# Three attentions of a fused transformer kernel: heads' score products on parts of TensorE's rows, units taken in pairs

## The chip, the cores and the metric

The kernel runs on one core of a Trainium2 chip. The metric is the device time of one execution in microseconds; the lower the better. All tensors are fp32.

## The reference

Sixteen images (84 x 84) are cut into 25 patches each and joined to 77 text tokens: 102 rows of 192 numbers for each of 16 sequences. Then come four pairs of an attention-like layer and a feed-forward layer, each on a layernorm and with a residual. Three of the four are softmax attentions with 12 heads:

```python
# first attention: grouped projections, relative positions
q, k: 12 heads of 64;  v: 12 heads of 16
probs = softmax((q + r_w) @ k.T + shift((q + r_r) @ r.T));  out = probs @ v @ Wo
# second (inside a layer with a convolution and a feed-forward): 12 heads of 16
attn = softmax(q @ k.T / 4);  out = attn @ v;  x = x + out @ attn_proj_w + attn_proj_b
# third: 12 heads of 64
attn = softmax(q @ k.T / 8);  out = attn @ v @ w_o + b_o
```

The others (soft-routed experts, two top-2 expert layers, a dense layer, a last attention without softmax) aren't touched by the change.

## The kernel before

Each layer runs in four **groups** (NG) of four sequences (GB). A row block has T = 102 rows, and a group's activations stand side by side as 408 columns. An attention's work in a group is cut into 16 **units** (UNITS): unit n belongs to sequence n // 4 and holds three heads (HPU). Five engines walk the units in step, each with its own hand-written loop, tied by semaphores; nothing reorders them. The passage of one unit, with the lines of the profile:

- TensorE makes the **scores** of three heads into one PSUM bank (L1928). An fp32 product shows as two records, so a unit's scores are "x6". Here the stationary operand is QT, 128 rows, in which the heads of several units stand above one another (two units of 64 rows; in the second attention four of 32). The moving operand is KZ, in which the keys of one unit stand at their rows and the other rows are zero. So all 128 rows take part in each product.
- VectorE takes each row's minimum (L929). The scores are scaled by a negative number, hence the minimum. In the first attention it first adds the relative positions (L923).
- ScalarE makes three exponentials with their sums (L1619), VectorE the inverse sums (L935), GpSimd multiplies (L666).
- TensorE **turns** (transposes) the three heads (L1967, one record each) into a bank of TBANKS, and ScalarE copies them to PT (L1613).
- TensorE multiplies with V, the **values** (L1957), into parts of 32 or 64 columns of the array. When a bank of them is full, VectorE copies it to OT (L945), and TensorE makes the **output product** of a sequence (L1940), in three parts.

ScalarE's order in step s of its loop is: copy unit s-4 to PT, then exponentials of unit s. The change leaves it as it is:

```python
                    if 0 <= s - 4 < UNITS:
                        k = at.bank(TBANKS)
                        src = full(k)[0:T, 0:TU].rearrange("p (h t) -> p h t", h=HPU)
                        free(activation(PT[s % 2][:, 0:HPU, :], src, ACT.Copy), k)
                    if s < UNITS:
                        ...
```

TensorE's order in its step s is: scores of unit s, a part of the output product, values of unit s-5, turn of unit s-3. The scores go round three banks in the second and third attention and wait for the exponentials of the unit that had the bank; in the first they go round two and wait for the addition.

In the first attention `pos(s)` puts **pieces** of other work beside the units: the position products of this and the next group (L2018; copied by ScalarE at L1661, behind the exponentials of unit s), the next group's transposes, queries and keys (L2010). ScalarE's pieces come behind unit s's exponentials. Its last group has few of them, and VectorE has pieces of the next layer instead.

The group's front (L1837 in the second and third attention) makes queries, keys and V. ScalarE copies the keys to KZ, each unit's rows apart (L1764: twelve copies of 32 rows in the second attention). GpSimd clears KZ ahead of each attention (L678, L760, L806). L1855 is the transposes with which the next group begins.

## Time and profile before

| | us |
|---|---|
| three runs | 1655.21, 1665.26, 1647.38 |
| median | 1655.21 |
| profiled execution, its own time | 1649.25 |
| its span from first to last instruction | 1647.5 |
| TensorE busy in the span | 1426.8 (87%) |
| VectorE, ScalarE, GpSimd busy | 684.2, 664.3, 387.5 |
| mean granted TensorE clock | 0.915 |

PE is TensorE's products, PEld its weight loads, DVE VectorE, ACT ScalarE, POOL GpSimd. A TensorE record spans the product from its start until its result has landed, so records overlap, and their starts tell the pace. In brackets behind a row of the timeline stands the idle time before it and the instruction that ended it.

### The profile page before, as it was taken

To read this page: it belongs to the slowest core of one execution; us is meant where nothing else is said; L and a number is where in the kernel's file an instruction comes from. 1 tells how busy PE (TensorE), PEld (TensorE's weight loads), DVE (VectorE), ACT (ScalarE), POOL (GpSimd) and SP (SyncE) were. 2 spreads that over 40 slices of the span, in tenths; PEclk is the share of its full clock that TensorE was granted. 3 is DMA by queue.
4 is the path that set the end of the run, shared out by engine and by line. 5 is a ranking of instruction groups with operands and counts; after the bars stand their busy time and mean duration, and the time that the engine had idled before them with its cause. 6 is when DMAs were issued, how large, how long until landed. Compare 5 with 4: busy or idle time off the path is not lost.

```text
span 1647.5 us, 31617 instructions
## 1 busy us (share of the span) xinstructions
PE 1426.8 (87%) x10268; PEld 1050.3 (64%) x10268; DVE 684.2 (42%) x2126; ACT 664.3 (40%) x2241; POOL 387.5 (24%) x468
## 2 busy tenths in 40 slices
PE   5899897788779678888998998799999999989994
PEld 3556665643334456666678898376676776879993
DVE  5567766611112765444326322344343323451113
ACT  1668665320001337777531122265455442213331
POOL 5213212300000232222101565122121100024441
PEclk9899997578877799999999899799999999889997
DMA  7433432649997000000005664200000300135553
GB/s 224 125 100 103 115 90 56 235 161 418 419 417 226 5 0 1 0 0 0 0 0 144 184 198 123 61 2 0 0 0 0 134 0 0 41 118 183 184 164 106
DMA packets 94439, 178.73 MB, mean 108 GB/s; under 512 B 35578, under 2 KB 54168, under 8 KB 92704
## 3 DMA queue, kind: packets, MB, share of 16 engines
q1 hardware_dynamic: 80144, 130.65, 25.2%
q10 hardware_dynamic: 7056, 30.67, 4.5%
q0 software_dynamic: 7136, 16.10, 3.2%
q8 instruction: 57, 0.93, 0.2%
q14 instruction: 46, 0.38, 0.1%
HBM read 150.39 MB, written 26.99 MB: 108 GB/s over the span
## 4 chain that ended last, share of the span: by engine, by line
PE 61%; issue 12%; DVE 12%; ACT 6%; DMA 6%; SPq 2%; POOL 1%; DVEq 0%; ACTq 0%; POOLq 0%
PE bank L1837 15%; PE bank L2357 6%; PE bank L2343 5%; PE bank L1928 4%; DMA AREA<-in_fc 4%; PE bank L1940 4%; PE bank L1957 3%; PE bank L2347 3%; PE bank L1967 3%; PE bank L2018 2%; PE bank L1903 2%; ACT ON L1619 2%; PE bank L2010 2%; PE bank L2274 1%; DVE MXU L929 1%
## 5 line engine op out<-in xcount | busy, mean ns | idle before, releaser
L1837 PE MATMUL bank<-XT,AREA 96*128 96x408 f32 (+1 forms) x640 | 239.4, 532 | 33.1 <-ACT XT L1573 15.7
L1837 PEld LDWEIGHTS bank<-XT,AREA 96*128 96x128 f32 (+1 forms) x640 | 121.9, 196 | 139.7 <-issue 100.1
L1928 PE MATMUL bank<-KZ,QT 128*102 128x102 f32 x1152 | 140.8, 262 | 9.0 <-ACT PB L1619 5.8
L666 POOL TENSOR_TENSOR PB<-PB,RCU 102x306 f32<-102x306 f32 x96 | 69.2, 720 | 317.0 <-DVE RCU L935 316.9
L650 POOL TENSOR_TENSOR RS<-VE,expo 102x4 f32<-102x4 f32 (+1 forms) x53 | 53.0, 1000 | 376.0 <-DVE VE L875 326.3
L1928 PEld LDWEIGHTS bank<-KZ,QT 128*102 128x102 f32 x1152 | 122.4, 174 | 27.2 <-issue 18.2
L2357 PE MATMUL bank<-WM,KZ 128*128 x660 | 118.2, 327 | 0.0
L2357 PEld LDWEIGHTS bank<-WM,KZ 128*128 128x128 f32 x660 | 105.7, 190 | 0.4
L1600 ACT ACTIVATE KZ<-bank,AREA 128x128 f32<-128x128 f32 x198 | 54.8, 375 | 121.7 <-PE bank L2347 121.7
L1940 PE MATMUL bank<-AREA,OT 128*102 128x192 f32 x384 | 88.9, 345 | 11.3 <-DVE SLOTS L1291 5.2
L1957 PE MATMUL bank<-PT,V 102*32 102x102 f32 (+1 forms) x1152 | 85.9, 270 | 14.5 <-DVE OT L945 12.3
L1613 ACT ACTIVATE PT<-bank 102x306 f32<-102x306 f32 x192 | 86.5, 452 | 26.2 <-PE bank L1967 25.7
L792 POOL DMA_INDIRECT rows_out<-KZ,TARGET x66 | 66.6, 1009 | 118.9 <-DVE KZ L1436 74.5
L666 POOL TENSOR_TENSOR ON<-ON,RCU 102x306 f32<-102x306 f32 x96 | 67.0, 698 | 92.4 <-DVE RCU L935 92.1
L1619 ACT ACTIVATE PB<-bank,MXU 102x102 f32<-102x102 f32 x192 | 65.9, 378 | 53.9 <-DVE MXU L929 53.9
L2343 PE MATMUL bank<-KZ,SLOTS 128*128 128x128 f32 x660 | 84.6, 275 | 2.6 <-issue 1.9
L2343 PEld LDWEIGHTS bank<-KZ,SLOTS 128*128 128x128 f32 x660 | 82.0, 192 | 3.4 <-issue 3.4
L780 POOL DMA_INDIRECT KZ<-rows_in,TOKEN x66 | 67.6, 1024 | 54.1 <-DVE TOKEN L1413 34.6
L1571 ACT ACTIVATE XT<-bank 96x408 f32<-96x408 f32 x56 | 25.8, 501 | 133.1 <-PE bank L1855 123.9
L929 DVE TENSOR_REDUCE MXU<-bank 102x3 f32<-102x306 f32 x128 | 61.0, 477 | 42.7 <-PE bank L1928 38.3
L1957 PEld LDWEIGHTS bank<-PT,V 102*32 102x32 f32 (+1 forms) x1152 | 43.2, 118 | 53.9 <-issue 34.4
L1732 ACT ACTIVATE QT<-bank 128x512 f32<-128x512 f32 (+1 forms) x32 | 15.7, 490 | 145.0 <-PE bank L2152 145.0
(335 smaller groups left out, 2734.3 us busy)
## 6 DMA issues: line engine op xcount, KB each, us to landing
AREA<-in_fc SPq DMA_DIRECT2D x10, 1536.0 KB, 21.5
SLOTS<-in_m3w SPq DMA_DIRECT2D x33, 384.0 KB
WM<-in_fc ACTq DMA_DIRECT2D x5, 2304.0 KB, 14.5
WM<-in_fc SPq DMA_DIRECT2D x6, 1536.0 KB, 21.2
AREA<-in_fc ACTq DMA_DIRECT2D x4, 2304.0 KB, 15.2
SLOTS<-in_m1w SPq DMA_DIRECT2D x33, 256.0 KB
AREA<-pos_scratch SPq DMA_DIRECT2D x16, 459.0 KB
pos_scratch<-AREA SPq DMA_DIRECT2D x8, 913.5 KB
```

The lines of the kernel that those rows point to most:

```text
L666: pool.tensor_tensor(p, p, scale, ALU.mult).then_inc(sem["probs_ready"], 1)
L780: pool.indirect_dma_start(XG[i % XRING], None, rows_in, bass.IndirectOffsetOnAxis(ap=TOKEN[:, i:i + 1], axis=0), bounds_check=NB * T - 1, ...
L792: pool.indirect_dma_start(rows_out, bass.IndirectOffsetOnAxis(ap=TARGET[:, i:i + 1], axis=0), YO[i % YRING], None, bounds_check=2 * NB * T ...
L929: give(dve.tensor_reduce(MXU[:, n % 4, 0:HPU], scores, AX.X, ALU.min), "probs_in")
L1613: free(activation(PT[s % 2][:, 0:HPU, :], src, ACT.Copy), k)
L1619: last = activation(p, p if pos else psum[k][0:T, cols(j)], ACT.Exp, scale=-1.0, bias=MXU[:, s % 4, j:j + 1], accum_out=SMU[:, s % 4, j:j ...
L1837: last = pe.matmul(dst, lhsT, rhs, start=n == 0, stop=n == len(pieces) - 1)
L1928: last = pe.matmul(psum[k][0:T, cols(j)], QT[:, tile, cols(bb)], KALL[:, unit % per_tile * (HEADS // per_tile) + tile, cols(bb)], start=Tr ...
L1940: last = pe.matmul(psum[PROJBANK][0:T, 0:D], OT[bb % 2][:, m, :], wo[:, m, :], start=m == 0, stop=m == parts - 1)
L1957: last = pe.matmul(psum[k][row:row + rows, cols(tile)], by_head(dv)[:, bb * HEADS + h, :], PT[n % 2][:, j, :], start=True, stop=True)
L2343: pe.matmul(p[:, c], w_all[:, (j * per + m) * 128:(j * per + m + 1) * 128], x[:, 0:TILE], start=m == 0, stop=False)
L2357: last = pe.matmul(p[:, 0:D], HG[i % HRING][:, f * 128:(f + 1) * 128], w2[:, bass.ds(e, 1), f * D:(f + 1) * D].rearrange("p o d -> p (o d) ...
```

## The change

Units are taken in pairs. A head's scores use only the rows at which its unit stands (64, or 32 in the second attention), of both operands; the products of the two units of a pair alternate, and go to different banks. The keys are copied whole (KT), and the zeros, their clearing and the waits for it are gone. TensorE's loop has twelve steps of a pair: values of pair step-3, turn of pair step-2, scores of pair step, then the pieces and the output product (in two parts). The scores have four banks in the second and third attention, two in the first; the values have one bank everywhere.

```diff
@@ names
-        STEPS = UNITS + 7
         PROJBANK = OBANKS[1]
-        SCORES, VALUES = (SBANKS + XBANKS[:1], SBANKS), (OBANKS[:1] + XBANKS[1:], OBANKS[:1])
+        PAIRS = UNITS // 2
+        PAIR_STEPS = PAIRS + 4
+        SCORES, VALUES = (SBANKS + XBANKS, SBANKS), OBANKS[0]
 ...
         def proj_step(bb, i):
-            return min(UPB * bb + UPB + 6 + i, STEPS - 1)
+            return min(UPB // 2 * (bb + 1) + 3 + i, PAIR_STEPS - 1)
@@ GpSimd: ahead of the first attention; two alike ahead of the second and third go too
-            for half in range(2):
-                pool.memset(KZ[64 - 64 * half:128 - 64 * half, half, :, :], 0.0
-                            ).then_inc(sem["halves_cleared"], at.one("halves_cleared"))
-            pool.wait_ge(sem["halves_cleared"], at.now("halves_cleared"))
@@ VectorE attention
-                for s in range(STEPS + 1):
-                    n = s - 6
-                    if 0 <= n < UNITS and av_filled(dv, n % UPB):
+                for s in range(2 * PAIR_STEPS):
+                    n = s - 5
+                    if s % 2 == 0 and 0 <= n < UNITS and av_filled(dv, n % UPB):
 ...
-                        if s - 1 == proj_step(bb, 2):
+                        if s == 2 * proj_step(bb, 1) + 1:
@@ ScalarE, second attention's keys (the first and third: two copies of 64 rows become one of 128)
                 for j in range(3):
                     k = at.bank(XBANKS)
-                    src = full(k)[:, 0:TG]
-                    for u in range(UPB):
-                        rows = slice(32 * u, 32 * u + 32)
-                        last = activation(KALL[rows, 3 * u + j, :], src[rows], ACT.Identity,
-                                          bias=bqk1[rows, 3 + j:4 + j])
-                    free(last, k)
+                    free(activation(KT[:, j, :], full(k)[:, 0:TG], ACT.Identity, bias=bqk1[:, 3 + j:4 + j]), k)
@@ TensorE attention, after
+                def values(pair):
+                    f = fill_of(dv, pair[0])
+                    if pair[0] == 0:
+                        moved(*v_moved)
+                    moved(pt_moved[pair[0]], pt_moved[pair[1]])
+                    if f >= 1 and (pair[0] % UPB == 0 or av_filled(dv, pair[0] % UPB - 1)):
+                        taken(f - 1)
+                    for n in pair:
+                        for j in range(HPU):
+                            h = HPU * (n % UPB) + j
+                            row, rows, tile, _ = av_place(dv, h)
+                            last = pe.matmul(psum[VALUES][row:row + rows, cols(tile)],
+                                             by_head(dv)[:, n // UPB * HEADS + h, :], PT[n % 2][:, j, :],
+                                             start=True, stop=True)
+                    if av_filled(dv, pair[1] % UPB):
+                        last.then_inc(sem["values_ready"], 1)
+                def turn(pair):
+                    for n in pair:
+                        pe.wait_ge(sem["probs_ready"], at.take("probs_ready"))
+                        k, p = claim(TBANKS)
 ...
+                def scores(pair):
+                    bb, dk = pair[0] // UPB, 128 // per_tile
 ...
+                    for j in range(HPU):
+                        for n in pair:
+                            rows = slice(n % per_tile * dk, n % per_tile * dk + dk)
+                            tile = n % UPB // per_tile * HPU + j
+                            last = pe.matmul(psum[banks[n % len(banks)]][0:T, cols(j)], QT[rows, tile, cols(bb)],
+                                             KT[rows, tile, cols(bb)], start=True, stop=True)
 ...
+                for step in range(PAIR_STEPS):
+                    pair_of = lambda n: (2 * n, 2 * n + 1) if 0 <= n < PAIRS else None
+                    if pair_of(step - 3):
+                        values(pair_of(step - 3))
+                    if pair_of(step - 2):
+                        turn(pair_of(step - 2))
+                    if pair_of(step):
+                        scores(pair_of(step))
                     if pos:
-                        pos(s)
+                        pos(2 * step)
+                    project_values(step)
+                    if pos:
+                        pos(2 * step + 1)
```

TensorE, second attention, a step within the loop over groups, before (units; ISA and REGISTER_ALU rows are waits with computed counts):

```order
L1957 MATMUL bank<-PT,V 32x102 x3
L1964 REGISTER_ALU
L1967 MATMUL bank<-ident,ON 102x102 x3
L1925 REGISTER_ALU
L1928 MATMUL bank<-KZ,QT 102x102 x3
```

and after:

```order
L1934 MATMUL bank<-KZ,QT 102x102 x12
L1915 ISA
L1796 ISA
L1918 MATMUL bank<-ident,PB 102x102 x3
L1915 REGISTER_ALU
L1796 REGISTER_ALU
L1918 MATMUL bank<-ident,PB 102x102 x3
L1929 REGISTER_ALU x2
L1934 MATMUL bank<-KZ,QT 102x102 x6
L1807 REGISTER_ALU x4
L1906 MATMUL bank<-PT,V 32x102 x6
```

The first row is the scores of pairs 0 and 1, then come the turn of pair 0, the scores of pair 2 and the values of pair 0: what was done for one unit is now done for two at a time, and the values wait for both copies of their pair.

ScalarE, second attention, end of a group's front and begin of its units, before:

```order
L1757 ACTIVATE QT<-bank,AREA 128x408
L1764 ACTIVATE KZ<-bank,AREA 32x408 x4
L1549 REGISTER_ALU
L1764 ACTIVATE KZ<-bank,AREA 32x408 x8
L1616 ISA
```

and after, with the first exponentials and copies, which stand in the same order as before:

```order
L1740 ACTIVATE QT<-bank,AREA 128x408
L1744 ACTIVATE KZ<-bank,AREA 128x408
L1533 REGISTER_ALU
L1744 ACTIVATE KZ<-bank,AREA 128x408 x2
L1600 ISA
L1603 ACTIVATE PB,SMU<-bank,MXU 102x102 x3
L1600 REGISTER_ALU
L1603 ACTIVATE PB,SMU<-bank,MXU 102x102 x3
```

Twelve key copies have become three; the units' copies (L1597) and exponentials (L1603) haven't moved against one another.

## Rows read from the trace of the kernel before

**Rows 1.** Windows of the second and third attention: length, busy time (instructions) by engine, PEclk, DMA, GB/s
```profile
718.00:754.00 36.00, 30.69 (x293) 22.86 (x293) 15.91 (x48) 29.69 (x125) 11.14 (x16) 1.00 0.00 0
1136.00:1170.00 34.00, 31.55 (x288) 25.85 (x287) 15.88 (x44) 23.43 (x113) 11.14 (x16) 1.00 0.00 0
```

**Rows 2.** Timeline, second attention, steady units: start, length, instruction, what idle time ended on
```profile
729.10 0.43 ACT L1613 ACTIVATE PT<-bank 102x306 f32<-102x306 f32 x1
...
729.59 0.38 PE L1957 MATMUL bank<-PT,V 102*32 102x102 f32 x6 [0.18 <-ACT PT L1613]
...
730.20 0.70 PE L1928 MATMUL bank<-KZ,QT 128*102 128x102 f32 x6
...
730.37 0.46 ACT L1613 ACTIVATE PT<-bank 102x306 f32<-102x306 f32 x1
...
730.88 0.38 PE L1957 MATMUL bank<-PT,V 102*32 102x102 f32 x6
...
731.19 0.47 PE L1967 MATMUL bank<-ident,ON 102*102 102x102 f32 x3
```

**Rows 3.** Timeline, second attention's third group: first scores, and the group's end
```profile
723.80 1.69 PEld L1928 LDWEIGHTS bank<-KZ,QT 128*102 128x102 f32 x18 [0.96 <-issue]
...
751.89 0.81 PEld L1855 LDWEIGHTS bank<-ident,XN 102*96 102x96 f32 x8
```

**Rows 4.** Timeline, same group: keys copied by ACT, and the product that waited
```profile
716.46 7.28 ACT L1764 ACTIVATE KZ<-bank,AREA 32x408 f32<-32x408 f32 x12 [0.77 <-PE bank L1837]
...
718.92 1.64 PE L1837 MATMUL bank<-XT,AREA 96*128 96x408 f32 x4 [1.13 <-ACT KZ L1764]
```

**Rows 5.** Timeline, third attention: first scores, the values, the transposes behind them
```profile
1135.50 0.17 PEld L1928 LDWEIGHTS bank<-KZ,QT 128*102 128x102 f32 x1 [0.15 <-issue]
...
1144.62 0.56 PE L1957 MATMUL bank<-PT,V 102*64 102x102 f32 x6
...
1145.11 0.47 PE L1967 MATMUL bank<-ident,PB 102*102 102x102 f32 x3
```

**Rows 6.** Timeline, third attention: from scores to the next copy
```profile
1152.47 0.70 PE L1928 MATMUL bank<-KZ,QT 128*102 128x102 f32 x6
...
1153.28 0.48 DVE L929 TENSOR_REDUCE MXU<-bank 102x3 f32<-102x306 f32 x1 [1.40 <-PE bank L1928]
...
1153.79 0.35 ACT L1619 ACTIVATE PB<-bank,MXU 102x102 f32<-102x102 f32 x1 [0.68 <-DVE MXU L929]
...
1154.77 0.43 ACT L1613 ACTIVATE PT<-bank 102x306 f32<-102x306 f32 x1
```

**Rows 7.** Timeline, third attention: end of the group
```profile
1169.95 0.82 PEld L1855 LDWEIGHTS bank<-ident,XN 102*96 102x96 f32 x8
```

**Rows 8.** Timeline, first attention: a position piece
```profile
156.71 0.94 PE L2018 MATMUL bank<-AREA 64*102 64x203 f32 x8
```

**Rows 9.** Timeline, first attention's last group: values, transposes, scores of one unit
```profile
259.89 0.56 PE L1957 MATMUL bank<-PT,V 102*32 102x102 f32 x6 [3.63 <-DVE OT L945]
260.38 0.75 PE L1967 MATMUL bank<-ident,ON 102*102 102x102 f32 x3
260.93 1.24 PE L1928 MATMUL bank<-KZ,QT 128*102 128x102 f32 x6
```

**Rows 10.** Windows with the granted clock, first attention
```profile
120.00:123.00 3.00, 1.57 (x14) 1.13 (x11) 1.89 (x5) 2.14 (x9) 0.43 (x1) 1.00 0.00 0
123.00:126.00 3.00, 3.00 (x21) 2.59 (x20) 1.13 (x3) 2.05 (x9) 0.27 (x1) 0.76 0.00 0
...
276.00:280.00 4.00, 2.95 (x23) 1.69 (x20) 2.62 (x9) 1.82 (x8) 1.39 (x2) 0.50 0.00 0
```

**Rows 11.** Chain that ended last, in order of time: start, length, what
```profile
28.53 5.05 DVE XN L1068 x4
...
614.28 5.25 DVE XN L879 x4
```

**Rows 12.** Timeline, GpSimd: the clearing ahead of the second attention
```profile
614.37 4.18 POOL L760 MEMSET KZ<- 128x4896 f32 x1
```

More of the change, by code:

```diff
@@ L802, in _ @@
             expert_rows(1)
-            for r in range(YRING):
-                pool.wait_ge(sem[f"scattered{r}"], 16 * len(range(r, TILES, YRING)))
-            for half in range(2):
-                pool.memset(KZ[64 - 64 * half:128 - 64 * half, half, :, :], 0.0
-                            ).then_inc(sem["halves_cleared"], at.one("halves_cleared"))
-            pool.wait_ge(sem["halves_cleared"], at.now("halves_cleared"))
             powers(1)
@@ L1916, in taken @@
                     pe.wait_ge(sem["values_taken"], before + f + 1)
-                for s in range(STEPS):
-                    if s < UNITS:
-                        bb, unit = s // UPB, s % UPB
-                        k = banks[s % len(banks)]
-                        if s < len(banks):
-                            pe.wait_ge(sem[f"bank_free{k}"], at.now(f"bank_full{k}") + 1)
-                        else:
-                            pe.wait_ge(sem[scores_read], at.take(scores_read))
+                def values(pair):
[6 more added lines that the diff above has]
+                    for n in pair:
@@ L1968, in attention @@
                         pt_moved[n] = filled(last, k)
+                def scores(pair):
+                    bb, dk = pair[0] // UPB, 128 // per_tile
+                    for n in pair:
+                        k = banks[n % len(banks)]
+                        if n < len(banks):
+                            pe.wait_ge(sem[f"bank_free{k}"], at.now(f"bank_full{k}") + 1)
+                        else:
+                            pe.wait_ge(sem[scores_read], at.take(scores_read))
+                    for j in range(HPU):
+                        for n in pair:
+                            rows = slice(n % per_tile * dk, n % per_tile * dk + dk)
+                            tile = n % UPB // per_tile * HPU + j
+                            last = pe.matmul(psum[banks[n % len(banks)]][0:T, cols(j)], QT[rows, tile, cols(bb)],
+                                             KT[rows, tile, cols(bb)], start=True, stop=True)
+                            if j == HPU - 1:
+                                last.then_inc(sem["scores_ready"], at.one("scores_ready"))
@@ new lines, in project_values @@
+                def project_values(step):
+                    for bb in range(GB):
+                        for i in range(2):
+                            if step != proj_step(bb, i):
+                                continue
+                            if i == 0:
+                                taken(fills(dv) * (bb + 1) - 1)
+                                claim(None, PROJBANK)
+                            half = (parts + 1) // 2
+                            for m in (range(half), range(half, parts))[i]:
+                                last = pe.matmul(psum[PROJBANK][0:T, 0:D], OT[bb % 2][:, m, :], wo[:, m, :],
+                                                 start=m == 0, stop=m == parts - 1)
+                            if i == 1:
+                                filled(last, PROJBANK)
@@ L2004, in _ @@
             moved(*r_moved[-2:])
-            pe.wait_ge(sem["halves_cleared"], at.take("halves_cleared", 2))
             def project(w, p6):
```

62 lines of the change are left out of this document (6 added, 56 removed).

## The prediction

> **What bounds the kernel now.** I read first the windows of the second and third attention [rows 1]: TensorE is busy 30.7 of 36 us and 31.6 of 34, ScalarE 29.7 and 23.4. TensorE seems to bound both. The timeline tells more. In the steady part of the second attention ScalarE's copies to PT follow each other at 729.10 and 730.37, 1.27 us apart, and TensorE's values at 729.59 and 730.88, 1.29 apart [rows 2]. So there a unit costs 1.27 on ScalarE (three exponentials and a copy, nothing between) and 1.29 on TensorE: both are full, and a unit can't get much cheaper through TensorE alone. In the third ScalarE has room, and TensorE sets the pace. A group's units, from the first scores to the next group's transposes, take 751.89 - 723.80 = 28.1 us in the second attention [rows 3] and 1169.95 - 1135.50 = 34.5 in the third [rows 5, 7].
>
> What lets the engines run side by side is distance. Before, the values of a unit wait for a copy that ScalarE made well before the exponentials whose scores come next on TensorE. I look at what the pairs do to that distance, since TensorE's queue is in order: who waits for a copy holds up the scores behind it.
>
> **TensorE's own work.** A unit's scores are six records in 0.70, the last one 0.25 long [rows 6], so (0.70 - 0.25) / 5 = 0.09 apart. In the first attention's position pieces eight products of 203 columns on 64 rows, by turns on the upper and the lower rows, take 0.94 [rows 8]. At the pace of the scores, doubled for twice the columns (0.18), eight in a row would take 7 x 0.18 + 0.33 = 1.6. So products on different rows do run at the same time, and a pair's scores should take what one unit's take: some 0.78 after a change of the operand's shape (0.70 and 0.08 for the first load, an estimate). The values of a unit take 731.19 - 730.88 = 0.31 to the transposes behind them [rows 2]. In a pair two heads share a part of 32 columns instead of one, about 0.22 more: 0.53. In the third attention 1145.11 - 1144.62 = 0.49 [rows 5] becomes some 0.70. Six transposes, at 0.09 with their drain, are 0.73. Sum of a pair: 0.53 + 0.73 + 0.78 = 2.04 us in the second attention, 2.21 in the third, against 2 x 1.29 = 2.6 for two units of the second before. Taken alone the change makes TensorE faster.
>
> **The wait that it adds.** In step k+2 TensorE does the values of pair k-1, then the turn of pair k, then the scores of pair k+2. The values wait for the copy of unit 2k-1. ScalarE makes that copy just before the exponentials of unit 2k+3, then come copy 2k, exponentials 2k+4, and copy 2k+1. Exponentials 2k+4 need the scores of pair k+2, which stand on TensorE behind the values that waited for copy 2k-1. And copy 2k+1, behind exponentials 2k+4, is what the next step's values wait for. That is a closed ring with nothing to spare: copy, values, turn, scores, minimum, exponentials, copy. Four banks don't help, since the scores are held by their place in the queue. Its length:
>
> - copy's end (729.10 + 0.43) to values: 729.59 - 729.53 = 0.06 [rows 2]
> - values, turn, scores: 2.04
> - scores' end to minimum, 1153.28 - 1153.17 = 0.11, minimum 0.48, on to ScalarE 0.03, exponentials 1154.77 - 1153.79 = 0.98, copy 0.43 [rows 6]: 2.03
>
> Together 4.13 us for a pair, against 2.6 before. ScalarE has 2.54 of work in it and idles 1.6; TensorE idles 2.1. In the third attention it is 4.30.
>
> **Second attention.** From the first scores: the exponentials of units 0 to 3 run as before, then copy 0, the exponentials of unit 4 (whose scores stand behind the turn of pair 0, which waits for GpSimd's second multiplication), then copy 1, at about 7.8 us (an estimate from these durations). Five rounds of the ring to copy 11: 7.8 + 5 x 4.13 = 28.4. Then two more values-turn-copy rounds, the last values, the copy to OT and the last output product, some 6.5. That is 34.9 against 28.1: +6.8. The front gets shorter. Twelve key copies of 0.61 (7.28) held the third key product until 718.92 [rows 4]; three copies hide behind products of 1.37 (4 passes at 0.34, an estimate from 1.64 for four with their tail [rows 4]). That is worth -2.1. Net +4.7 a group, +19 for four, at full clock.
>
> **Third attention.** First part 8.2, five rounds 21.5, tail 8: 37.7 against 34.5, +3.2 a group, +13 for four. The output products now lie in TensorE's idle time, which is why it loses less. Twelve key copies of 64 rows become six there. I take them as hidden behind the front's products and give them nothing; without that cover six fewer at 0.61 [rows 4] would be worth 3.7 a group, up to -15 for four.
>
> **First attention.** There the ring has the addition in it too (0.5, an estimate by the minimum's 0.48), and the piece behind the first unit's exponentials: the second piece of a step waits for banks that ScalarE empties only then, and is itself ahead of the next values. The ring is then 4.13 + 0.5 + 0.94 for the piece [rows 8] and its copy's start, some 6.1 a pair. Pieces and units tied each other before as well (a unit's piece waits for the copies behind the last unit's exponentials), so I reckon only some 0.5 a pair more, 4 a group, of which the tail and the key copies give 1 back. +3 a group for three groups and +4 for the last, in which VectorE's pieces fall into the ring, is about +12. It is my coarsest term: between -5 and +30.
>
> **Clearing.** VectorE's normalisation ahead of the second attention lasts 5.25 for four [rows 11] while GpSimd clears KZ, 4.18 from the same moment [rows 12]; the one at the start lasts 5.05. Without the clearing some 3.5 each should go: -7, between 0 and -8. The third I take at 0, within the same bounds.
>
> **The clock.** In 120 to 123 us TensorE was busy 1.57 of 3 us, and behind that the granted clock fell to 0.76 for the next three [rows 10]. In 276 to 280 it stayed at 0.50, that is 1.2 of 2.4 GHz, with 2.95 of 4 busy [rows 10]. The ring leaves TensorE busy 2.04 of 4.13, so I expect that it falls. At 1.2 GHz a unit's values, turn and scores take 0.49, 0.55 and 1.24 [rows 9]; for a pair I make 0.83 + 1.24 + 1.24 = 3.3, and the ring is 5.4. Low throughout, a group of the second attention gets 5 x 1.27 longer, its tail and the next front some 6 more: +17, +68 for four. In the third the output products would fill TensorE's idle time and may bring the clock back: low for three rounds +6 a group, throughout +15. I take half of the low price in the second, 4 x 11 = +44, and +24 in the third.
>
> **Sum.** 12 + 44 + 24 - 7 = +73 on the profiled execution's 1649.25: 1722. The median of the runs is 6 above it and their spread 18, so I say 1725.
>
> **Rivals.**
>
> - *The clock holds.* 12 + 19 + 13 - 7 = +37: 1686. For it: 2.1 us of idle time in each ring is broken up by output products from the fifth step on. Against: [rows 10].
> - *The clock is low throughout*, in the first attention also (25): 25 + 68 + 60 - 7 = +146: 1795.
> - *Rows don't run together.* The change then doesn't do what it says. A pair's scores cost 0.54 more in the ring, about 20 rings a stage (five to seven in four groups) and three stages: 75 x 0.54 = 40 more, 1765. [Rows 8] speak against it.
> - *The ring doesn't close, ScalarE becomes the bound, and it is faster.* If copies ran far enough ahead of the values, a pair would cost ScalarE's 2.54: the second attention keeps its pace and gains the front's 2.1 and some 3 of output products, 5 x 4 = 20; the third would come to about 27, 7.5 x 4 = 30; the first 8, the clearing 7: -65, 1584. It decides itself at 2.6 us a pair; the ring would have to lose 1.5, and its parts outside TensorE alone are 2.1. For it: TensorE's sum of 2.04. Against: the order of ScalarE's loop, which is unchanged.
>
> On this last rival bears the Trainium skill, page "TensorEngine Tiling (Array Packing)", section "PSUM Bottleneck": tiling speeds up TensorE but not the emptying of PSUM, which may become the bottleneck. By that rule the second attention would stand at ScalarE's 1.27 a unit, with no loss; the trace shows ScalarE full already, and my ring says that it will have gaps instead.
>
> **Chances.** A measurement of this kernel tells about 1% from no change. Ring with a mixed clock 0.52 (1700 to 1755); clock holds 0.20 (1670 to 1700); low throughout 0.12 (1755 to 1800); no concurrency 0.04; ring much shorter or made up elsewhere, within 1%, 0.08; faster by over 1% 0.04. The range leaves out the fastest and part of the slowest: 1665 to 1790. Slower by over 1%: 0.88.
>
> **What would show it.** In the trace of after: in the second attention, copies to PT in groups of two about 4.1 us (or 5.4) apart in steady steps; ScalarE idle until VectorE's minimum, once a pair; TensorE idle until ScalarE's copy ahead of the values; a pair's scores in 0.8 us, with two banks' records starting together; PEclk under 1.00 there; ScalarE's busy share down. The first key copy of the second attention followed at once by products; no 5 us normalisation at 28 and 614. Wrong would prove me scores that don't wait behind the values, or a ring under 3 us.

## The result, and the profile after

| | before | after |
|---|---|---|
| median of the runs, us | 1657.7 (1647.38 to 1665.26) | 1775.31 |
| ratio, 95% interval | | 1.0703 (1.0624 to 1.0782) |
| profiled execution: its own time, span | 1649.25, 1647.5 | 1769.63, 1767.9 |
| mean granted TensorE clock | 0.915 | 0.834 |

The change makes the kernel 7% slower. One execution of after took 3294.63 us and is left out of the ratio, though not of the median; the three others took 1769.63 to 1776.12.

I cut both spans at the first attention's first scores (L1928 before, L1934 after) and, for the second and third attention, at the transposes (L1855, L1831) with which their first group begins; each attention ends at the first transposes behind its last group. All in us:

| stretch | before | after | more | predicted |
|---|---|---|---|---|
| to the first attention's first scores | 62.6 | 55.7 | -6.9 | -3.5 |
| first attention | 225.8 | 258.6 | +32.8 | +12 |
| to the second attention | 331.3 | 328.9 | -2.4 | -3.5 |
| second attention | 175.3 | 232.1 | +56.8 | +44 |
| to the third | 245.8 | 248.3 | +2.5 | 0 |
| third attention | 254.4 | 295.7 | +41.3 | +24 |
| rest | 352.3 | 348.6 | -3.7 | 0 |
| sum | | | +120.4 | +73 |

Windows of after over a group's units, second and third attention; columns as in [rows 1], to which they answer (the engines stand there in the order PE, PEld, DVE, ACT, POOL):

```profile
656.00:701.00 45.00, 32.31 (x265) 23.75 (x264) 14.03 (x41) 23.88 (x113) 11.13 (x16) 0.58 0.01 1
1156.00:1200.00 44.00, 32.14 (x284) 25.75 (x283) 15.81 (x44) 23.65 (x113) 11.14 (x16) 0.73 0.00 1
```

Before, TensorE and ScalarE had little room in the second attention: they were busy 30.69 and 29.69 of 36 us. Now TensorE is busy 32.31 of 45 and ScalarE 23.88, and the granted clock is 0.58 and 0.73 in place of 1.00. Both engines idle, so something waits in turn. The timeline of the second attention of after, rows of one round and the start of the next (they answer to [rows 2, 6]):

```profile
724.94 1.36 PE L1934 MATMUL bank<-KZ,QT 32*102 32x102 f32 x12
726.40 0.48 DVE L914 TENSOR_REDUCE MXU<-bank 102x3 f32<-102x306 f32 x1 [3.57 <-PE bank L1934]
...
726.91 0.35 ACT L1603 ACTIVATE ON<-bank,MXU 102x102 f32<-102x102 f32 x1 [1.95 <-DVE MXU L914]
...
727.89 0.43 ACT L1597 ACTIVATE PT<-bank 102x306 f32<-102x306 f32 x1
...
728.37 0.89 PE L1906 MATMUL bank<-PT,V 102*32 102x102 f32 x12 [2.07 <-ACT PT L1597]
...
729.19 1.26 PE L1918 MATMUL bank<-ident,PB 102*102 102x102 f32 x6
...
730.38 1.36 PE L1934 MATMUL bank<-KZ,QT 32*102 32x102 f32 x12
731.84 0.48 DVE L914 TENSOR_REDUCE MXU<-bank 102x3 f32<-102x306 f32 x1 [2.06 <-PE bank L1934]
...
733.89 0.90 PE L1906 MATMUL bank<-PT,V 102*32 102x102 f32 x12 [2.15 <-ACT PT L1597]
```

Read it as a circle. ScalarE idles 1.95 until VectorE's minimum; VectorE waited for the scores, and those stood on TensorE behind the values, which idled 2.07 until ScalarE's copy. The values come 733.89 - 728.37 = 5.52 us apart for a pair, against 2 x 1.29 before. The pair's twelve score records end in 1.36 together. In the chain that ended last the same beat shows (start, length, what):

```profile
665.52 3.53 issue
...
670.98 3.53 issue
...
676.43 3.60 issue
```

670.98 - 665.52 = 5.46. Between these rows stand only GpSimd's multiplications and short pieces of issue, no output product and no DMA. In the third attention the beat is 5.92 (values at 1170.43 and 1176.35). The normalisations of [rows 11] no longer run beside a clearing. Before, one of the four instructions at 614.28 took 4.38 us, the others 0.37 each, while GpSimd cleared KZ from 614.37 for 4.18 [rows 12]. Now:

```profile
28.05 1.40 DVE L1053 TENSOR_SCALAR XN<-H,MV,RS 102x192 f32<-102x192 f32 x4 [1.15 <-POOL RS L650]
...
641.80 1.25 DVE L864 TENSOR_SCALAR XN<-SLOTS,MV,RS 102x192 f32<-102x192 f32 x4 [1.12 <-POOL RS L650]
```

### The profile page after: what moved, and what is told of

Its sections match the earlier page's. It is cut to its first block, busy times and chain, and to the rows that moved or that the text cites. A ratio compares the mean times of both kernels' runs of the same rounds, so it can differ in the third digit from the quotient of the medians.

```text
span 1767.9 us, 31591 instructions
## 1 busy us (share of the span) xinstructions
PE 1454.3 (82%) x10268; PEld 1076.5 (61%) x10268; DVE 669.1 (38%) x2114; ACT 630.3 (36%) x2169; POOL 374.7 (21%) x463
## 4 chain that ended last, share of the span: by engine, by line
PE 42%; issue 32%; DVE 8%; DMA 6%; ACT 5%; POOL 4%; SPq 2%; POOLq 0%; DVEq 0%; ACTq 0%
PE bank L2349 6%; PE bank L1813 5%; DMA WM<-in_fc 5%; PE bank L2335 4%; PE bank L1934 4%; PE bank L1918 3%; PE bank L2339 3%; PE bank L2006 3%; PE bank L1906 2%; PE bank L2014 2%; POOL PB L666 1%; DVE MXU L914 1%; ACT ON L1603 1%; ACT PB L1603 1%; PE bank L1950 1%
## 5 line engine op out<-in xcount | busy, mean ns | idle before, releaser
L1906 PE MATMUL bank<-PT,V 102*32 102x102 f32 (+1 forms) x1152 | 81.4, 330 | 84.6 <-ACT PT L1597 82.3
L1906 PEld LDWEIGHTS bank<-PT,V 102*32 102x32 f32 (+1 forms) x1152 | 53.4, 150 | 123.4 <-issue 93.3
L1934 PE MATMUL bank<-KZ,QT 64*102 64x102 f32 (+1 forms) x1152 | 108.4, 345 | 0.0
L1950 PE MATMUL bank<-AREA,OT 128*102 128x192 f32 x384 | 99.3, 395 | 5.5 <-DVE H L1482 2.4
L1597 ACT ACTIVATE PT<-bank 102x306 f32<-102x306 f32 x192 | 79.9, 424 | 66.2 <-PE bank L1918 65.1
L1934 PEld LDWEIGHTS bank<-KZ,QT 64*102 64x102 f32 (+1 forms) x1152 | 89.4, 239 | 20.8 <-issue 18.1
L1603 ACT ACTIVATE PB<-bank,MXU 102x102 f32<-102x102 f32 x192 | 64.4, 355 | 96.5 <-DVE MXU L914 96.5
L2014 PE MATMUL bank<-AREA 64*102 64x203 f32 x384 | 67.5, 404 | 27.3 <-ACT AREA L1644 17.6
L1950 PEld LDWEIGHTS bank<-AREA,OT 128*102 128x102 f32 x384 | 69.3, 203 | 20.6 <-issue 9.1
L1603 ACT ACTIVATE ON<-bank,MXU 102x102 f32<-102x102 f32 x192 | 64.4, 355 | 43.5 <-DVE MXU L914 43.5
```

Source lines behind the costliest of these rows:

```text
L1603: last = activation(p, p if pos else psum[k][0:T, cols(j)], ACT.Exp, scale=-1.0, bias=MXU[:, s % 4, j:j + 1], accum_out=SMU[:, s % 4, j:j ...
L1906: last = pe.matmul(psum[VALUES][row:row + rows, cols(tile)], by_head(dv)[:, n // UPB * HEADS + h, :], PT[n % 2][:, j, :], start=True, stop ...
L1934: last = pe.matmul(psum[banks[n % len(banks)]][0:T, cols(j)], QT[rows, tile, cols(bb)], KT[rows, tile, cols(bb)], start=True, stop=True)
L1950: last = pe.matmul(psum[PROJBANK][0:T, 0:D], OT[bb % 2][:, m, :], wo[:, m, :], start=m == 0, stop=m == parts - 1)
L2014: last = pe.matmul(p[0:T, j * NREL:(j + 1) * NREL], head(QR, h, 2, 64, cols(bb)), head(RT, h, 2, 64, slice(0, NREL)), start=True, stop=True)
```

## The experiments

The ring can be seen; what lowers the clock can't. The theories: **A**, products on part of the rows lower the granted clock by themselves; **B**, only the gaps of the ring lower it; and for the order, that the ring accounts for the whole loss. Each run is compared with runs of the kernel before on the same chip; the clock is that of its profiled execution. f1_pairs_all_rows, f2_before_whole_keys and f3_open_all_rows leave out the zeros and so sum other heads too: they tell times alone.

| run | what | median us | ratio (95%) | clock |
|---|---|---|---|---|
| e1_copies_paired | after, copies of a pair together | 1692.86 | 1.024 (1.0172 to 1.0309) | 0.84 |
| e6_copies_pieces | and pieces one place later | 1659.01 | 1.0045 (1.0011 to 1.0079) | 0.87 |
| e3_rows_alone | before, scores on part of the rows | 1850.93 | 1.1214 (1.1144 to 1.1284) | 0.786 |
| e2_filler_clock | after, five unread products a pair | 1722.57 | 1.0444 (1.0377 to 1.051) | 0.892 |
| f1_pairs_all_rows | after, all rows | 1744.29 | 1.0542 (1.0498 to 1.0586) | 0.884 |
| f2_before_whole_keys | rows alone, all rows | 1633.7 | 0.9881 (0.984 to 0.9922) | 0.915 |
| f3_open_all_rows | e6, all rows | 1626.74 | 0.9834 (0.9793 to 0.9876) | 0.917 |
| f4_open_zeros_second | e6, zeros in the second | 1646.82 | 0.9952 (0.9924 to 0.998) | 0.889 |
| g1_open_filler | e6, two unread products a pair | 1620.84 | 0.9815 (0.9779 to 0.9852) | 0.914 |
| g2_open_zeros_two | e6, zeros in second and third | 1639.74 | 0.9927 (0.9899 to 0.9955) | 0.903 |
| h1_rows_alone_filler | rows alone, one unread product a unit | 1767.8 | 1.056 to 1.081, each of its runs over the median before | 0.874 |
| h2_open_filler_one | e6, one unread product a pair | 1656.26 | 0.9998 (0.9961 to 1.0035) | 0.87 |

### Opening the ring

e1_copies_paired makes both copies of a pair ahead of its exponentials, so that the values no longer wait behind an exponential that needs later scores:

```diff
-                    if 0 <= s - 4 < UNITS:
+                    for m in (s - 4, s - 3) if s % 2 == 0 else ():
+                        if 0 <= m < UNITS:
```

> The changed kernel, but ScalarE makes the two copies to PT of a pair together, ahead of the pair's exponentials, in all three attentions; TensorE's order is untouched. Theory (a closed ring through the values' wait for the second copy): copy 2k+1 no longer stands behind exponentials 2k+4, the ring opens, and a pair in the second attention costs what ScalarE has to do, 2.5 to 2.8 us, against 5.45 in the trace of after; the granted clock there goes back to about 1.00; a group of the second attention goes from 58.0 to about 41 us, one of the third from 72.8 to about 60. The first attention keeps its ring through the pieces and gains little. Total about 1650 (1635 to 1675). Rival 1 (TensorE's work on parts of the rows is slow by itself, shape changes and all): order on ScalarE changes nothing, the total stays above 1750. Rival 2 (the clock falls for another reason than the gaps): the ring opens but the clock stays low, a pair costs 3.3 or more, total about 1710.

Measured 1692.86: 82 of the 118 us come back. That is less than forecast (1635 to 1675), because the clock did not: it is rival 2, the ring open and the clock low, with 1710. e6_copies_pieces is that, and TensorE's pieces of the first attention one place later, so that none waits ahead of the values for a bank that ScalarE empties behind them:

```diff
                     if pos:
-                        pos(2 * step)
+                        pos(2 * step - 1)
                     project_values(step)
                     if pos:
-                        pos(2 * step + 1)
+                        pos(2 * step)
```

> As the kernel with the copies of a pair together, and TensorE's pieces of the first attention one place later: behind the scores of pair k come pieces 2k-1 and 2k, not 2k and 2k+1, so that the piece that waits for ScalarE's emptied banks is no longer ahead of the values of the next step in the same breath. Theory (the first attention's ring goes through exponentials 2k, their piece's copies, piece 2k+1, values, turn, scores): the ring opens, a group of the first attention goes from 66.8 to 53 to 58 us, total 30 to 45 us under the kernel with paired copies, about 1610. Rival (the first attention is bound by something else, the fixed pieces' DMAs or TensorE's own work at a low clock): its period stays above 64, total within 10 us of the kernel with paired copies.

1659.01: 34 more, inside the 30 to 45 forecast; the total of about 1610 had counted on the first step's full gain. The first attention's groups, from 66 to 67 us in after, fall to 52 to 58, and its last, 58.2, to 47.1. So the order of the copies and of the pieces was the greater part of the loss. But the second attention's units still took 33.0 to 37.5 against 28.1. TensorE of e1_copies_paired there:

```profile
715.07 1.36 PE L1935 MATMUL bank<-KZ,QT 32*102 32x102 f32 x12
716.36 0.90 PE L1907 MATMUL bank<-PT,V 102*32 102x102 f32 x12
717.19 1.61 PE L1919 MATMUL bank<-ident,PB 102*102 102x102 f32 x6
718.73 1.36 PE L1935 MATMUL bank<-KZ,QT 32*102 32x102 f32 x12
```

and windows of its units (columns as in [rows 1]):

```profile
706.00:742.00 36.00, 32.16 (x263) 23.01 (x262) 14.02 (x41) 23.54 (x113) 11.14 (x16) 0.57 0.00 0
```

No row has idle time ahead of it, a pair comes every 718.73 - 715.07 = 3.66 us, and the clock is 0.57. The ring is open, TensorE is the bound, at nearly half speed. Gaps don't keep the clock low here. They may have started it: it fell at the group's start, in the pause of 2.58 us ahead of the first turn at 709.75.

### Rows alone, and one line put back

e3_rows_alone is the kernel before (its order, its units one by one) with keys copied whole, no clearing, and this:

```diff
-                            last = pe.matmul(psum[k][0:T, cols(j)], QT[:, tile, cols(bb)],
-                                             KALL[:, unit % per_tile * (HEADS // per_tile) + tile, cols(bb)],
+                            dk = 128 // per_tile
+                            rows = slice(unit % per_tile * dk, unit % per_tile * dk + dk)
+                            last = pe.matmul(psum[k][0:T, cols(j)], QT[rows, tile, cols(bb)],
+                                             KT[rows, tile, cols(bb)], start=True, stop=True)
```

> The kernel before, its units one by one, with only this of the change: scores on their own rows, keys copied whole, no clearing. Theory (the pairs' order costs the time, not the rows): nothing is lost in the order; won are some 7 us of clearing, 2.1 us of key copies in each of four groups of the second attention and some in the first; lost is one more change of the operand's shape a unit (about 0.15 us, wherever TensorE sets the pace, so 2 us a group): total 1640 to 1660, the second attention's period 41 to 44 and the third's 63 to 66. Rival 1 (products on parts of the rows are the cost): total above 1700.

The miss of the study: 1850.93, slower than the whole change. Its windows of units in the second and third attention, and TensorE in steady units:

```profile
677.00:724.00 47.00, 44.35 (x264) 29.40 (x264) 14.02 (x41) 24.26 (x113) 11.13 (x16) 0.55 0.00 1
...
1184.00:1239.00 55.00, 52.42 (x284) 39.17 (x282) 15.56 (x44) 24.38 (x113) 11.13 (x16) 0.60 0.00 1
```

```profile
803.90 0.75 PE L1944 MATMUL bank<-ident,ON 102*102 102x102 f32 x3
804.58 1.36 PE L1906 MATMUL bank<-KZ,QT 32*102 32x102 f32 x6
805.87 0.56 PE L1934 MATMUL bank<-PT,V 102*32 102x102 f32 x6
806.36 0.75 PE L1944 MATMUL bank<-ident,ON 102*102 102x102 f32 x3
807.04 1.36 PE L1906 MATMUL bank<-KZ,QT 32*102 32x102 f32 x6
```

TensorE is busy 44.35 of 47 us, row follows row, and the clock is 0.55: near the lower of its two levels, 1.2 GHz of 2.4. A unit takes 2.46. The Trainium skill, page "TensorE: Matmul & The Clock Gate", section "HAM oscillation — how this bites in real kernels", lays a falling clock to idle gaps between bursts and advises to keep TensorE busy. The trace agrees with one half of this. The fall stands behind a pause at the group's start, as in every group of this run's second and third attention. But behind it TensorE is busy nearly all the time, and the clock stays at the low level for 43 us, until the next group's front:

```profile
797.00:801.00 4.00, 2.45 (x29) 1.98 (x26) 2.46 (x7) 3.15 (x19) 1.39 (x2) 0.99 0.00 0
801.00:844.00 43.00, 41.90 (x235) 27.39 (x234) 11.14 (x33) 21.11 (x95) 9.74 (x14) 0.50 0.00 0
```

f2_before_whole_keys tests the rows with one line, which puts the products of e3_rows_alone on all rows again:

```diff
-                            rows = slice(unit % per_tile * dk, unit % per_tile * dk + dk)
+                            rows = slice(0, 128)
```

> The kernel before in its own order, unit by unit, with the keys copied whole, no clearing, and score products on all 128 rows without zeros (a head's scores also sum the other heads in the same columns, so the values are not the reference's). It differs from the run with rows alone (1850.93) in one line: which rows the score products use. Theory A: the clock is that of the kernel before (0.915), and what is left is the gain of the fewer key copies and of the clearing: 1650 - 7 - 4 x 2.1 = 1634, down to 1620 if the first and third attention's key copies were not hidden. Theory B (something else in that run was slow: the copies whole, the missing clearing, bank or port conflicts of whole keys): 1800 to 1850 again.

1633.7: 217 us from one line, to the forecast of theory A. Its windows, same stages:

```profile
667.00:695.00 28.00, 25.13 (x264) 18.45 (x263) 14.03 (x41) 22.79 (x113) 11.14 (x16) 1.00 0.00 0
...
1054.00:1088.00 34.00, 31.58 (x287) 25.72 (x286) 15.87 (x44) 23.38 (x113) 11.14 (x16) 1.00 0.01 2
```

As many instructions (x264 and x264 of TensorE), and 28 us in place of 47, clock 1.00 in place of 0.55. Theory A stands, and B falls as the only cause. Zeros have no part in it: the kernel before has them and f2_before_whole_keys has not, and both show 1.00. f2_before_whole_keys has pauses at the start of its second attention's groups too (0.82 and 0.35 us, where e3_rows_alone has 1.20 and 0.35), and no fall behind them. The run also prices what the change wins besides: whole keys and no clearing are worth some 20 of 1653.

### The same line in the change, ring closed and open

f1_pairs_all_rows and f3_open_all_rows put the same line into after and into e6_copies_pieces.

> The kernel after, with each score product on all 128 rows of QT and KT again (one line). The keys are still copied whole and there are no zeros, so a head's scores also sum the other heads that stand in the same columns: the values are not the reference's, the count, shape and order of the instructions are those of the kernel before for the scores, of the kernel after for all else. Theory A (products on part of the rows lower the granted clock by themselves): the clock comes back to nearly 1.00 in the second attention's units, though the ring is closed and each pair's scores take about 0.54 us more (12 records one behind the other). The ring is then 4.7 us, a group's units in the second attention about 38 us against 45.1, in the third about 41 against 44.9; total about 1725. Theory B (the ring's gaps lower the clock, the rows have nothing to do with it): the clock stays at 0.68 in the second attention's group, the scores cost 1.24 more at that pace in each ring, total 1815 to 1840.

> The run with paired copies and shifted pieces (1659.01), with each score product on all 128 rows, keys whole, no zeros (a head's scores also sum the other heads in the same columns; the values are not the reference's). Ring open and clock restored at once. Theory A: a group's units in the second attention fall from 33.0 to 37.5 to about 28.5, as before the change, in the third they stay near 33 (TensorE has 0.54 more a pair but a full clock); total 1659 - 4 x 7 = 1631, between 1615 and 1640. Theory B (the second attention's units were long for the order of the pairs, not the clock): 0.54 more a pair over 24 pairs a group set, total 1659 to 1700.

f1_pairs_all_rows gave 1744.29, 19 more than theory A: the clock rose only to 0.83 in the second attention's units (0.58 in after) and to 0.78 in the third's (0.73):

```profile
708.00:748.00 40.00, 27.08 (x263) 22.73 (x262) 14.04 (x41) 23.59 (x113) 11.13 (x16) 0.83 0.00 0
1200.00:1246.00 46.00, 34.65 (x285) 30.28 (x284) 15.89 (x44) 23.60 (x113) 11.14 (x16) 0.78 0.00 0
```

Here all products are on all rows and TensorE idles 13 of 40 us. So the gaps lower the clock as well. But here it comes back in the same group, while the ring still turns and TensorE is busy little more than half of the time:

```profile
715.00:722.00 7.00, 4.25 (x32) 3.59 (x30) 2.35 (x7) 3.46 (x18) 1.78 (x3) 0.59 0.00 0
736.00:743.00 7.00, 3.92 (x52) 3.24 (x52) 2.96 (x10) 5.20 (x27) 2.78 (x4) 1.00 0.00 0
```

In after it stays at 0.50 from 664 to 696, to the end of the group's units. f3_open_all_rows has neither ring nor parts: 1626.74, the second attention's units 29.3 to 30.5, the third's 32.4 to 33.6, close to theory A. In its second attention, too, the clock falls behind the pause at the start, and is back at 1.00 by 673, where e3_rows_alone stays low for 43 us:

```profile
669.00:673.00 4.00, 4.00 (x35) 3.42 (x34) 1.31 (x4) 3.22 (x16) 1.48 (x3) 0.57 0.00 0
673.00:687.00 14.00, 12.77 (x152) 10.07 (x151) 7.66 (x22) 11.99 (x63) 6.27 (x9) 1.00 0.00 0
```

From these medians the order (copies and pieces together) costs 1744.29 - 1626.74 = 118 with all rows and 1775.31 - 1659.01 = 116 with parts; the parts cost 31 with the ring closed, 32 with it open, and 217 where units come one by one. The account closes: f3_open_all_rows lies 27 under the kernel before on its chip (1653.45), the order adds 118 and the parts 31, together 122, and the change measured 118. The medians of the kernel before, of the result and of the experiments' four chips, lie between 1649.15 and 1657.7, so a difference of medians from two chips is good to some 8.

### More work, less time

If products on all rows hold the clock, unread ones should pay. e2_filler_clock adds to after, behind each pair's scores in the second and third attention, five of these into a bank that the next scores overwrite:

```diff
+                    for f in range(5):
+                        pe.matmul(psum[k][0:T, 0:2 * T], QT[:, f % 3, 0:T], KT[:, f % 3, 0:2 * T],
+                                  start=True, stop=True)
```

> The changed kernel with extra work that nothing reads: in the second and third attention, behind the scores of each pair but the last, five products of 102 by 204 on 128 rows (about 1.7 us at 2.4 GHz) into a bank that TensorE owns at that time. They lie where TensorE waits for ScalarE's copy, and keep it busy. Theory (half of the loss in these attentions is the low clock that the ring's gaps bring, and not the ring itself): the granted clock goes to about 1.00, the ring in the second attention from 5.45 to 4.1 to 4.3 us, its group from 58.0 to 47 to 49, the third's from 72.8 to 65 to 67: total about 1705, faster with more work. Rival (the clock has no part in it): the ring stays or grows by the extra products, total 1775 or more.

1722.57: 53 us faster than after by the medians, 43 by the ratios, for more work (forecast 1705). And it shows the ring at full clock:

```profile
715.76 0.54 PE L1906 MATMUL bank<-PT,V 102*32 102x102 f32 x12 [0.16 <-ACT PT L1597]
716.24 0.73 PE L1918 MATMUL bank<-ident,ON 102*102 102x102 f32 x6
716.90 0.79 PE L1954 MATMUL bank<-KZ,QT 32*102 32x102 f32 x12
717.62 1.97 PE L1940 MATMUL bank<-KZ,QT 128*102 128x204 f32 x10
719.75 0.55 PE L1906 MATMUL bank<-PT,V 102*32 102x102 f32 x12 [0.17 <-ACT PT L1597]
...
723.82 0.55 PE L1906 MATMUL bank<-PT,V 102*32 102x102 f32 x12 [0.24 <-ACT PT L1597]
```

3.99 and 4.07 us a pair, the values each time still waiting for ScalarE's copy, and the scores of a pair in 0.79. The next two pairs, with an output product behind the unread ones, take 4.41 and 4.17 with no wait: there TensorE's own work fills the ring. h1_rows_alone_filler does it to the rows alone, one such product ahead of each unit's scores.

> The run with rows alone (order of the kernel before, no ring, products on 32 and 64 rows, 1850.93) plus one unread product of 102 x 204 on all 128 rows ahead of each unit's scores in the second and third attention. It adds 0.35 us of TensorE work a unit, 45 us in 128 units, and no wait. Theory A (products on part of the rows let the granted clock fall though TensorE has no gaps, and products on all rows hold it): the clock goes from about 0.5 to near 1.00 in the units, a group's units from 47.2 to 28.2 + 5.6 = 34 in the second attention and from 57 to 34.3 + 5.6 = 40 in the third: total 1851 - 53 - 68 = 1730; if one such product a unit is too little, between that and 1850. Theory B (the time is in the products on part of the rows themselves): 1851 + 45 = 1896 or more.

Its median, 1767.8, is 83 below the rows alone. In the profiled run the third attention is at clock 1.00 with units of 41.5 (forecast 40, from 57), the second at full clock in two groups, 35.0, and at the low one in the two others, 55.5 and 58.2. The four runs lie between 1745.07 and 1786.87, so by how much it wins is uncertain (64 to 106 us), not that it does. This run also shows a fall with no pause ahead of it. In the second attention's first group TensorE is busy without a gap from 634 on; about 5 us behind the first scores, at 646.8, the clock falls and stays low. A full group follows:

```profile
634.00:646.00 12.00, 12.00 (x60) 8.33 (x59) 5.16 (x14) 5.08 (x18) 1.00 (x2) 1.00 0.01 2
648.00:692.00 44.00, 44.00 (x228) 28.96 (x227) 10.15 (x30) 18.73 (x89) 9.47 (x14) 0.50 0.00 1
711.00:746.00 35.00, 33.70 (x295) 22.96 (x296) 13.65 (x40) 24.16 (x113) 11.14 (x16) 1.00 0.00 0
```

### Looking for a version that wins

Two ways to spare the clock with the ring open: the form of before (keys beside zeros, all rows), or unread products. f4_open_zeros_second and g2_open_zeros_two take the first, as in the kernel before, on top of e6_copies_pieces; g1_open_filler and h2_open_filler_one the second, with `range(2)` and `range(1)` in the loop above.

> The run with paired copies and shifted pieces (1659.01), with the form of before (keys in KZ with zeros, twelve key copies of 32 rows, its clearing by GpSimd, all 128 rows) in the second attention alone. The first and third keep products on 64 rows. It computes what the reference does. Theory A: the second attention's group goes back to about 43.3 us from 46 to 49.5 (its clock to 1.00; the key copies cost 2.1 of what is won), the clearing comes back with 4: 1659 - 4 x 5 + 4 = 1643, and it would be level with the kernel before or 0.5% ahead. Theory B: no change or slower by the copies and the clearing, 1660 to 1675.

> The run with paired copies, shifted pieces and the form of before in the second attention (1646.82), with that form in the third as well: products on all 128 rows, keys beside zeros, two key copies of 64 rows, the clearing by GpSimd. Only the first attention keeps products on 64 rows. It computes what the reference does. If the rows are what keeps the third attention's units at 35.6 (against 32.5 in the run with the open ring and all rows), four groups win 3 us each: 1647 - 12 = 1635, 1 to 1.3% ahead of the kernel before. If the key copies or the clearing are not hidden in the third attention, up to 3.7 a group is lost again: 1650.

> The run with paired copies and shifted pieces (1659.01; products on 32 and 64 rows) plus two products of 102 x 204 on all 128 rows behind each pair's scores in the second and third attention, into a bank that the next scores overwrite, read by nobody. About 0.75 us more TensorE work a pair. If products on part of the rows lower the granted clock and products on all rows hold it, the clock in the second attention goes from 0.76 to near 1.00 and the units from 33.0 to 37.5 down to 30, in the third to 32.5, as in the run with all rows and the open ring (1626.74): total 1626 to 1640, faster for more work. If the filler is just work: 22 pairs' worth a group pair set, up to 0.75 more for each of 8 pairs in 8 groups, 48 us: 1660 to 1707.

> The run with paired copies, shifted pieces and a filler of two unread products a pair (1620.84), with one product in place of two: 0.37 us less TensorE work a pair. If one holds the clock as well, TensorE has a little more room and the third attention, which TensorE sets, wins up to 8 x 0.37 = 3 a group: 1610 to 1621. If one is too little, the clock falls in part and the time goes back towards that without a filler, 1659: 1625 to 1650.

1646.82 and 1639.74 came within 5 of the forecasts: 0.5 and 0.7% under the kernel before. g1_open_filler is the fastest of all that compute what the reference does: 1620.84, 5 under its forecast, 1.9% under the kernel before (the interval ends at 0.9852) and, by the two ratios, 8.3% under after. Its windows and TensorE's rows in the second attention:

```profile
662.00:691.00 29.00, 26.31 (x294) 19.53 (x293) 14.16 (x42) 22.93 (x113) 11.13 (x16) 1.00 0.00 0
```

```profile
713.81 0.55 PE L1907 MATMUL bank<-PT,V 102*32 102x102 f32 x12
714.29 0.82 PE L1919 MATMUL bank<-ident,PB 102*102 102x102 f32 x6
715.03 0.79 PE L1955 MATMUL bank<-KZ,QT 32*102 32x102 f32 x12
715.75 0.94 PE L1941 MATMUL bank<-KZ,QT 128*102 128x204 f32 x4
716.62 0.55 PE L1907 MATMUL bank<-PT,V 102*32 102x102 f32 x12
```

A pair in 716.62 - 713.81 = 2.81 us, where e1_copies_paired had 3.66 with some 0.8 less to do; units are 28.8 in the second attention and 32.9 in the third. One product a pair is too little to rely on: h2_open_filler_one measured 1656.26, above both of its forecasts. Its profiled run, the slowest of its twelve (1668.78), had units of 40.7 at clock 0.57 in one group and 34.5 at 0.76 in the next; over the twelve the mean clock lies between 0.87 and 0.887, over g1_open_filler's six between 0.906 and 0.915. To turn and score ahead of the values in TensorE's step wasn't tried.

## Why the prediction was right, and where it was not

The sign, the mechanism and the range held: 1775 lies within 1665 to 1790. The likeliest case's own range, 1700 to 1755, did not hold it; by size the result belongs to the rival in which the clock is low throughout (1755 to 1800), to which I gave 0.12. No large term cancelled another: all three attentions lost more than I had put, and it is the range's width on the slow side that held the result. The sum had a slip too, without effect: 1722 and the 6 to the median are 1728, not 1725.

- **TensorE's own work.** A pair's scores 0.78 predicted, 0.79 measured at full clock. At the low clock twelve records of a pair take the 1.36 that six of one unit take in e3_rows_alone. The rival that rows don't run together falls.
- **The ring.** 4.13 predicted, 3.99 and 4.07 measured at full clock (e2_filler_clock); 5.4 at the low one, 5.46 and 5.52 measured. It breaks where the order of ScalarE's copies is changed, as it should.
- **The front and the clearing.** From a group's transposes to its first scores 752.1 to 767.1 before, 701.3 to 714.2 after: -2.1, as predicted. The normalisations got 3.65 and 4.0 shorter, predicted 7 in all, but less of it reached the span: the transposes behind the first start 2.1 earlier (31.72 for 33.83), and the stretch to the second attention is 2.4 shorter. Most of the other 4.8 us of the first stretch wasn't in my sum: the products ahead of the first scores met a higher granted clock (1.00 from 32 to 55.7; before 0.79 from 34 to 42 and 0.75 from 50 to 62.6), and the last sixteen of them take 1.60 in place of 2.96.
- **The clock, the step that was off.** "The ring leaves TensorE busy 2.04 of 4.13, so I expect that it falls", and then "I take half of the low price in the second". The fall came, the mixture didn't: 0.58 over the units in the second attention, where a group cost 14.2 more and I had put 11 (17 low throughout). In the third the clock was mixed, 0.73, and a group cost 10.3 more where I had put 6 (15 throughout). For the gaps alone the idea was sound: in f1_pairs_all_rows, the same ring with all rows, the clock falls and then comes back to 1.00 as the output products join, and the total is 1744.29, inside my 1700 to 1755. What the prediction didn't have is that products on part of the rows keep the clock low once it has fallen (e3_rows_alone, after) and can bring it down with no gap (h1_rows_alone_filler). The row that I drew on, [rows 10], shows a fall behind idle time and can't show the other cause, since before no scores were on part of the rows. [Rows 8], position products on 64 rows, I read for their pace only.
- **The first attention.** +32.8 against +12, outside its bounds of -5 to +30. The ring through the pieces is worth about 34 (e1_copies_paired to e6_copies_pieces). Two units took 5.3 to 7.3 us before (values at 136.98, 144.30, 150.10, 156.00 and 161.26), a pair takes 6.6 to 9.2 in after (147.47, 156.71, 164.11, 170.70 and 178.10). I had reckoned 0.5 a pair more, because units and pieces had tied each other before; over these four it is 1.6. The clock took part: windows over three groups' units show 0.76 to 0.83, before 1.00, and 0.62 in the last group, before 0.75.
- **The rival in which the ring doesn't close,** 1584, could be built: g1_open_filler is that kernel with the clock held. ScalarE's copies of a pair then come 2.81 us apart (715.56 and 718.37) with no idle time between them. ScalarE, which reads the scores and the turned heads from PSUM, may then become the bound, as the Trainium skill's page "TensorEngine Tiling (Array Packing)", section "PSUM Bottleneck", has it; the trace agrees as far as ScalarE is full, but TensorE's rows, the unread products among them, follow each other as well, so that it isn't shown which of the two sets the pace. The run gives 1620.84 and not 1584: 2.81 a pair and not 2.54, and, as far as I can tell, the filler takes the room that TensorE had in the third attention.

Open stays why one unread product holds the clock in some groups and not in others of the same run, whether the falls of e3_rows_alone needed the pause ahead of them, how the first attention's loss divides between ring and clock, and what moved the stretches that the change doesn't touch by +2.5 and -3.7.

## What to carry to other kernels

When work is taken in larger lots, follow one lot round all engines' queues: if engine X waits for Y's copy, and Y's copy stands behind work that needs X's next product, the lot costs the whole circle, however idle both look. Put the copy ahead of that work first, and change the lots second. And when a product is moved to part of the rows, read the granted clock before its duration: in this kernel a shape that saves array rows halved the pace of all that stood around it, and then a product that nobody reads paid for itself.

## What the runs showed of the hardware that I had not expected

- With scores on 32 or 64 rows the granted clock of a stretch was 0.55 and 0.60 while TensorE was busy 44.35 of 47 and 52.42 of 55 us; with the same instructions on all rows it was 1.00. In the whole kernel that is 217 us.
- Behind a pause the clock fell with all rows too, but was back within 4 us (f3_open_all_rows); with part of the rows it stayed low for 43 (e3_rows_alone), and once it fell though TensorE had been busy without a gap (h1_rows_alone_filler at 646.8).
- One normalisation on VectorE took 4.38 us beside GpSimd's clearing of 4.18 us, and 0.37 without it.
- The gain of concurrent rows is real and small here: at full clock a pair's scores take 0.79 in place of 1.24 (twelve records on all rows, f1_pairs_all_rows at 734.52).
- Adding some 0.8 us of unread products a pair in two attentions shortened the kernel from 1659.01 to 1620.84.
